# Key sums of two groups in the opening of a four-layer kernel: features on ScalarE, two products in PSUM, masks on GpSimd

## The chip, the core and the metric

The kernel is one program on one NeuronCore of a Trainium2 chip. Its engines are TensorE (PE, with its weight loads PEld), VectorE (DVE), ScalarE (ACT), GpSimd (POOL) and SyncE (SP, which here issues most DMAs). Each engine takes its instructions in program order and waits at semaphores. The metric is the device time of one execution in microseconds, lower is better.

## What is computed

There are 16 sequences of 128 tokens with 256 channels (`x`), and a context of the same shape. Four blocks follow one another, each with a residual and a tanh gate:

```python
x = x + tanh(g_xattn[0]) * L0_xattn(layernorm(x), ctx)   # WKV scan over tokens
x = x + tanh(g_ffn[0])   * L0_ffn(layernorm(x))          # MLP + product-key experts (PEER)
x = x + tanh(g_xattn[1]) * L1_xattn(layernorm(x), ctx)   # linear attention, 16 heads
x = x + tanh(g_ffn[1])   * L1_ffn(layernorm(x))          # 8 experts, top 2, + a shared one
```

The change touches the key side of the linear attention, which depends on the context and on weights alone and so can be computed at any time before the attention:

```python
kvp = kv @ Wkv.T;  k, v = split(kvp, 2)
k = where(k > 0, k + 1.0, exp(k))               # features
kv_summary = einsum('bhsd,bhse->bhde', k, v)    # per head, over the tokens
k_sum = k.sum(axis=-2)
```

## The kernel before

The 16 sequences are handled in four groups of four. `wkv_*` works in WKV groups (0, 1, 2, 3 hold sequences 0 to 3, 8 to 11, 4 to 7, 12 to 15); `mlp`, `attn` and `moe` in main groups.

**The order** is written out by hand. `START` (line 128) is a list of steps `kind group part`, then come four passes `("mlp", f)`, one for each main group, of 12 units and a tail, and `PLAN` (line 133) names the steps that follow each unit. `LAST` closes. Every engine walks the same list `SCHED` and issues its own share of each step, so the list fixes the order on every engine and in every DMA queue. The opening is what stands before the first unit: layer norms, the scans of groups 0 and 1 (`wkv_in`, `wkv_out`), the high and low parts of the first weight blocks (`split`), and a little of `kv`.

**`kv g t`** makes the key sums of one sequence. PE multiplies context by `wkv` into a PSUM bank (L766: key and value, two matmuls of 128x512 in fp32). ACT reads it three times (L1022 to L1024): `k_e` = exp(k), `k_r` = relu(k), and the values into `v_x`, which has 8 columns of ones behind each 128. DVE forms min(k_e, 1) + k_r in place (L1266). At the next part, PE multiplies `k_e` by `v_x` (L775, two matmuls of 128x136, 16 heads' products and the sums at once), and DVE takes the result out of PSUM times `head_mask` into `kv_sum` (L1272), since only the blocks of one head with itself are wanted. `k_e`, `k_r` and `v_x` have two buffers each.

In the list before, sequence 0 and the keys of sequence 1 stand in the opening; group 0 is finished behind units 1 and 2 of the first MLP; group 1 stands behind units 8 to 10 and the start of the second MLP; group 2 behind units 1 to 5 of the second; group 3 behind its units 9 to 12.

**What surrounds it.** An MLP unit below 8 is twelve fp32r matmuls of 512 columns (L636 to L638: three passes, two halves, A and B), a Silu on ACT (L1098), a product on DVE (L1390), and `down` three units later (L660). From unit 8 on the PEER part needs the routes: a long DVE chain (`route g 2` to `8`, L1279 to L1343) ends in transposes and in `exps_t_l` (L1361), for which PE waits with L726. The same DVE queue carries the scans (L1237), reciprocals (L1249), residuals (L1205), layer norm statistics (L1179) and the normalized input (L1201). POOL computes the reciprocal root (L1601, L1596), the low parts of weights (L1566) and parts of the scan's output (L1610 to L1618). PE uses six PSUM banks `ring` in turn. SP loads contexts 2 and 3 behind `kv 0 4` and `kv 1 4`, with `wqg` and `wo` behind the latter, and a weight block behind every `split`.

## Time and profile before

| | us |
|---|---|
| three runs | 518.77, 519.91, 523.19 |
| median | 519.91 |
| span of the profiled execution | 517.5 |

Engine busy time in that span, and the span in 40 slices of 12.9 us:

```profile
PE 449.8 (87%) x2142; PEld 355.1 (69%) x2142; DVE 360.9 (70%) x1034; ACT 246.7 (48%) x452; POOL 154.5 (30%) x156
## 2 busy tenths in 40 slices
PE   1617999599999889999999999898999799899991
PEld 1315688368578666878778886787777588788851
DVE  6896779995289986565987966978867554531173
ACT  3618574363576346346125315470453454955540
POOL 3955342330002131110000001032336014477771
PEclk9966999799999989999999999999999999999997
```

Each digit is the busy share of a slice in tenths; PEclk is the granted clock of TensorE. The first three or four slices are the opening, where PE stands at 1, 6, 1 and 7 tenths while DVE works; from the fifth slice to the last but a few PE is at 9, with gaps at slices 8 (5 tenths) and 14 and 15 (8 tenths). The first unit of the first MLP starts at 43.4 us.

### The profile page before, as it was taken

To read this page: it belongs to the slowest core of one execution; us is meant where nothing else is said; L and a number is where in the kernel's file an instruction comes from. 1 tells how busy PE (TensorE), PEld (TensorE's weight loads), DVE (VectorE), ACT (ScalarE), POOL (GpSimd) and SP (SyncE) were. 2 spreads that over 40 slices of the span, in tenths; PEclk is the share of its full clock that TensorE was granted. 3 is DMA by queue.
4 is the path that set the end of the run, shared out by engine and by line. 5 is a ranking of instruction groups with operands and counts; after the bars stand their busy time and mean duration, and the time that the engine had idled before them with its cause. 6 is when DMAs were issued, how large, how long until landed. Compare 5 with 4: busy or idle time off the path is not lost. (4 is left out here: it accounts for less than half of the span.)

```text
span 517.5 us, 7233 instructions
## 1 busy us (share of the span) xinstructions
PE 449.8 (87%) x2142; PEld 355.1 (69%) x2142; DVE 360.9 (70%) x1034; ACT 246.7 (48%) x452; POOL 154.5 (30%) x156
## 2 busy tenths in 40 slices
PE   1617999599999889999999999898999799899991
PEld 1315688368578666878778886787777588788851
DVE  6896779995289986565987966978867554531173
ACT  3618574363576346346125315470453454955540
POOL 3955342330002131110000001032336014477771
PEclk9966999799999989999999999999999999999997
DMA  8500312000300000960000000123232423346394
GB/s 303 187 31 30 103 31 83 0 1 0 101 2 0 2 0 14 310 178 0 1 1 1 1 0 2 32 71 102 90 115 83 123 73 91 114 139 208 85 385 153
DMA packets 32965, 42.00 MB, mean 81 GB/s; under 512 B 3483, under 2 KB 26781, under 8 KB 32928
## 3 DMA queue, kind: packets, MB, share of 16 engines
q1 hardware_dynamic: 28224, 32.28, 20.7%
q0 software_dynamic: 3744, 8.42, 4.4%
q10 hardware_dynamic: 960, 0.86, 0.5%
q8 instruction: 18, 0.29, 0.2%
q14 instruction: 19, 0.16, 0.1%
HBM read 24.97 MB, written 18.39 MB: 84 GB/s over the span
## 5 line engine op out<-in xcount | busy, mean ns | idle before, releaser
L660 PE MATMUL acc<-w_down,act_s 128*128 128x256 f32 x384 | 92.2, 387 | 0.9 <-DVE act_s L1386 0.9
L660 PEld LDWEIGHTS acc<-w_down,act_s 128*128 128x128 f32 x384 | 74.6, 195 | 13.2 <-DVE act_s L1386 1.3
L636 PE MATMUL ring<-xt_h,up_l 128*128 128x512 f32 x160 | 70.5, 441 | 2.9 <-DVE xt_l L1356 1.5
L1601 POOL TENSOR_TENSOR rstd<-var_eps,minus_half 128x4 f32<-128x4 f32 x14 | 14.9, 1068 | 176.5 <-DVE var_eps L1186 176.5
L637 PE MATMUL ring<-xt_l,up_h 128*128 128x512 f32 x160 | 63.8, 399 | 0.0
L638 PE MATMUL ring<-xt_h,up_h 128*128 128x512 f32 x160 | 63.7, 398 | 0.0
L1098 ACT ACTIVATE act_s<-ring 128x512 f32<-128x512 f32 x48 | 28.6, 597 | 59.9 <-PE ring L638 59.6
L631 PE MATMUL ring<-small,xn 128*128 128x128 f32 x160 | 23.6, 297 | 26.2 <-ACT xn L998 14.1
L699 PE MATMUL ring<-up_e,act_s 128*128 x184 | 44.3, 383 | 2.3 <-issue 2.0
L1637 POOL DMA_INDIRECT x_rows<-main_a,slots x32 | 31.1, 971 | 43.7 <-ACT main_a L1119 34.8
L1390 DVE TENSOR_TENSOR act_s<-ring,act_s 128x512 f32<-128x512 f32 x32 | 22.0, 686 | 30.8 <-PE ring L638 21.0
L631 PEld LDWEIGHTS ring<-small,xn 128*128 128x128 f32 x160 | 20.1, 153 | 29.6 <-ACT xn L998 14.9
L699 PEld LDWEIGHTS ring<-up_e,act_s 128*128 128x128 f32 x184 | 33.1, 190 | 7.1 <-issue 3.5
L636 PEld LDWEIGHTS ring<-xt_h,up_l 128*128 128x128 f32 x160 | 30.5, 191 | 10.5 <-DVE xt_l L1356 1.8
L638 PEld LDWEIGHTS ring<-xt_h,up_h 128*128 128x128 f32 x160 | 30.5, 191 | 7.3
L637 PEld LDWEIGHTS ring<-xt_l,up_h 128*128 128x128 f32 x160 | 30.6, 191 | 7.0 <-issue 1.4
L1098 ACT ACT_TABLE_LOAD x21 | 26.9, 1283 | 0.4
L1205 DVE SCALAR_TENSOR_TENSOR x_nat<-ring,small,x_nat 128x512 f32<-128x512 f32 x24 | 18.0, 749 | 11.2 <-PE ring L893 7.7
L1179 DVE BATCH_NORM_STATS2 stats<-x_nat 128x6 f32<-128x256 f32 x64 | 22.4, 413 | 4.7 <-DMA x_nat<-in_x 4.3
L1645 POOL DMA_INDIRECT y_rows<-act_s,block_home x16 | 15.9, 994 | 30.3 <-ACT act_s L1156 25.6
L726 PE MATMUL ring<-exps_t_l,sel_exps 128*128 128x512 f32 x24 | 13.5, 564 | 9.9 <-DVE exps_t_l L1361 5.3
L1543 DVE TENSOR_TENSOR pairs<-ring,pairs 128x256 f32<-128x256 f32 x12 | 5.1, 423 | 23.3 <-ACT pairs L1139 23.3
(275 smaller groups left out, 987.8 us busy)
## 6 DMA issues: line engine op xcount, KB each, us to landing
main_b<-x_rows SPq DMA_DIRECT2D x22, 257.0 KB, 2.8
x_rows<-v_t SPq DMA_DIRECT2D x1, 3983.5 KB, 16.7
up_l<-y_rows SPq DMA_DIRECT2D x5, 512.0 KB, 7.0
stage<-in_w_mlp SPq DMA_DIRECT2D x8, 256.0 KB, 2.6
up_e<-in_w_moe SPq DMA_DIRECT2D x8, 256.0 KB, 2.6
x_rows<-v_t SPq DMA_DIRECT2D x1, 1927.5 KB, 22.8
x_nat<-in_x SPq DMA_DIRECT2D x7, 256.0 KB, 7.7
out_x<-x_nat SPq DMA_DIRECT2D x6, 256.0 KB, 5.2
```

Of the source, the lines that this page charges most:

```text
L631: last = pe.transpose(bank[:, t * P:(t + 1) * P], xn[n % 2][:, t, c * P:(c + 1) * P], ident)
L636: pe.matmul(out, wl, xh, start=first, stop=False, skip_group_check=True)
L637: pe.matmul(out, wh, xl, start=False, stop=False, skip_group_check=True)
L638: return pe.matmul(out, wh, xh, start=False, stop=final, skip_group_check=True)
L660: last = pe.matmul(acc[t // 2][:, t % 2, :], act_s[n % RING][:, tok], w_down[:, u, :], start=u == 0 and t % 2 == 0, stop=final, skip_group ...
L699: last = pe.matmul(bank[:, j * 2 * P:(j + 1) * 2 * P], x_block_t[n % 2][:, c, j * P:(j + 1) * P], up_e[:, bass.ds(e * UP + c * 2 * P, 2 * ...
L1098: act.activation(act_s[n % RING][:, :], bank[:, :], ACT.Silu).then_inc(free_sem((step, "A", u)), 1)
L1179: last = dve.bn_stats(stats[:, n, t, :], x_nat[:, b, :])
L1205: return dve.scalar_tensor_tensor(out, bank, gates[:, gate:gate + 1], out, ALU.mult, ALU.add)
L1390: free((step, "B", u), dve.tensor_tensor(s[:, :], bank[:, :], s[:, :], ALU.mult))
L1637: pool.indirect_dma_start(x_rows[group_of(g)], bass.IndirectOffsetOnAxis(ap=slots[:, t, k:k + 1], axis=0), to_send[n % SENDS], None).then_ ...
L1645: pool.indirect_dma_start(y_rows, bass.IndirectOffsetOnAxis(ap=block_home[:, n, j:j + 1], axis=0), y_blocks[n % RESULTS][:, j * D:(j + 1) ...
```

## The change

The list of `kv` steps moves one stage ahead: groups 0 and 1 (`OPEN_KV = 2`) are both finished in the opening, group 2 takes the places of group 1, and the places that group 2 had in the second MLP stay empty. `split 0 0` and `split 0 1` stand later in the opening. For the first two groups the features are made on ACT alone, and PE adds the two halves in PSUM. For all groups ACT takes the product out of PSUM unmasked, and POOL applies the mask in `kv_sum` afterwards, in new steps `mask`.

```diff
+OPEN_KV = 2
-START = """wkv_in 0 0, setup 0 0, wkv_in 0 1, wkv_in 1 0, wkv_in 0 2, split 0 0, wkv_out 0 0, wkv_in 1 1, wkv_out 0 1, wkv_in 1 2,
-    wkv_out 0 2 3, split 0 1, kv 0 0, wkv_out 0 4 5, kv 0 1, wkv_out 1 0, wkv_out 0 6 7, x_stats 0 0, wkv_out 1 1, mlp_in 0 0 1,
-    wkv_out 1 2, mlp_in 0 2, wkv_out 1 3 4"""
+START = """wkv_in 0 0, setup 0 0, wkv_in 0 1, wkv_in 1 0, wkv_in 0 2, wkv_out 0 0, kv 0 0, wkv_in 1 1, kv 0 1, wkv_out 0 1,
+    wkv_in 1 2, wkv_out 0 2, kv 0 2, wkv_out 0 3 4, kv 0 3, wkv_out 0 5, split 0 0, kv 0 4, kv 1 0, split 0 1, kv 1 1,
+    wkv_out 1 0, wkv_out 0 6 7, kv 1 2, x_stats 0 0, wkv_out 1 1, kv 1 3, mlp_in 0 0 1, kv 1 4, wkv_out 1 2, mlp_in 0 2,
+    wkv_out 1 3 4"""
...
-        2: "wkv_out 1 6 7, x_stats 1 0, kv 0 2",
+        2: "wkv_out 1 6 7, x_stats 1 0, mask 0 0 1 2 3",
...
@@ PE, kind kv @@
+                        opening = g < OPEN_KV
+                        if opening:
+                            pe.wait_ge(open_k_ready, n + 1)
+                        else:
+                            pe.wait_ge(k_ready, n - OPEN_KV * GT + 1)
...
+                            own = slice(c * P, (c + 1) * P)
+                            last = pe.matmul(bank[:, c * KVW:(c + 1) * KVW], k_e[n % 2][:, own], v_x[n % 2][:, c, :],
+                                             start=True, stop=not opening)
+                            if opening:
+                                last = pe.matmul(bank[:, c * KVW:(c + 1) * KVW], k_r[n % 2][:, own], v_x[n % 2][:, c, :],
+                                                 start=False, stop=True)
@@ ACT, kind kv @@
+                        if g < OPEN_KV:
+                            act.activation(k_e[n % 2][:, :], bank[:, 0:D], ACT.Relu, scale=-1.0).then_inc(k_clipped, 1)
+                        else:
+                            act.activation(k_e[n % 2][:, :], bank[:, 0:D], ACT.Exp)
...
+                        if g < OPEN_KV:
+                            act.wait_ge(k_clipped, n + 1)
+                            act.activation(k_e[n % 2][:, :], k_e[n % 2][:, :], ACT.Exp, scale=-1.0).then_inc(open_k_ready, 1)
+                    if t > 0:
+                        bank = full(act, (step, "V", t - 1))
+                        act.activation(kv_sum[:, wkv_seqs(g)[t - 1], :], bank[:, 0:C * KVW],
+                                       ACT.Copy).then_inc(free_sem((step, "V", t - 1)), 1)
@@ DVE @@
-                        free((step, "V", t - 1), dve.tensor_tensor(
-                            kv_sum[:, seqs[t - 1], :].rearrange("p (c m) -> p c m", c=C),
-                            bank[:, 0:C * KVW].rearrange("p (c m) -> p c m", c=C),
-                            head_mask.unsqueeze(1).broadcast_to([P, C, KVW]), ALU.mult))
+                elif kind == "kv" and g >= OPEN_KV and part < GT:
...
@@ POOL @@
+                elif kind == "mask":
+                    own = kv_sum[:, wkv_seqs(g)[part], :].rearrange("p (c m) -> p c m", c=C)
+                    pool.wait_ge(later_loaded, 16)
+                    freed(pool, (("kv", g), "V", part))
+                    pool.tensor_tensor(own, own, head_mask.unsqueeze(1).broadcast_to([P, C, KVW]),
+                                       ALU.mult).then_inc(sums_masked, 1)
```

exp(-relu(-k)) is min(exp(k), 1), so that `k_e` and `k_r` together are the same feature as before. The masks of group 0 stand behind unit 1 and those of group 1 behind unit 4 of the first MLP, those of groups 2 and 3 behind units 1 and 11 of the second. PE waits for all 16 masks once, at the first attention.

How the order moves, at three places. ACT at the end of the opening, before: `er_pad` and `xt_f_pad` are scan data of group 1, `xn` is the input of the first MLP, `xt_h` its transposed high part.

```order
L984 ACTIVATE xt_f_pad<-xt_f_pad,own_weight 128x4x128
L998 ACTIVATE xn0<-x_nat,shift2,rstd2 128x256 x4
L984 ACTIVATE er_pad<-er_pad,own_weight 128x4x128
L1014 ACTIVATE xt_f_pad<-xt_f_pad,own_weight 128x4x128
L1051 ACTIVATE xt_h<-ring3 128x512
L1051 ACTIVATE xt_h<-ring4 128x512
L1014 ACTIVATE er_pad<-er_pad,own_weight 128x4x128
```

The same place of ACT now, from the features of the last sequence on:

```order
L1038 ACTIVATE k_e1<-ring1 128x256
L1041 ACTIVATE k_r1<-ring1 128x256
L1042 ACTIVATE v_x1<-ring1 128x2x128
L1046 ACTIVATE k_e1<-k_e1 128x256
L1049 ACTIVATE kv_sum<-ring2 128x272
L1012 ACTIVATE xn0<-x_nat,shift2,rstd2 128x256 x4
L1049 ACTIVATE kv_sum<-ring5 128x272
L998 ACTIVATE er_pad<-er_pad,own_weight 128x4x128
L1028 ACTIVATE xt_f_pad<-xt_f_pad,own_weight 128x4x128
L1076 ACTIVATE xt_h<-ring3 128x512
L1076 ACTIVATE xt_h<-ring4 128x512
L1028 ACTIVATE er_pad<-er_pad,own_weight 128x4x128
```

Two sequences of features came in ahead of `xn` (one is shown), and one eviction of `kv_sum` between `xn` and what follows.

PE behind the first unit of the second MLP, before (`q_pad` and `gate_pad` hold the route's input):

```order
L775 MATMUL ring4<-v_x0,k_e0 128x136 x2
L775 MATMUL ring5<-v_x1,k_e1 128x136 x2
L785 MATMUL ring0<-q_pad,later 128x512
L785 MATMUL ring0<-gate_pad,later 128x512
L766 MATMUL ring1<-wkv,v_t0 128x512
L766 MATMUL ring1<-wkv,v_t1 128x512
L636 MATMUL ring2<-xt_h,up_l 128x512
```

Now:

```order
L785 MATMUL ring0<-v_x0,k_e0 128x136 x2
L785 MATMUL ring1<-v_x1,k_e1 128x136 x2
L798 MATMUL ring2<-q_pad,later 128x512
L798 MATMUL ring2<-gate_pad,later 128x512
L641 MATMUL ring3<-xt_h,up_l 128x512
```

The key product of group 2 is gone between the route's product and the next unit.

DVE at the same stretch, before (L1279 begins the route's chain):

```order
L1272 TENSOR_TENSOR kv_sum<-ring4,later 128x272
L1272 TENSOR_TENSOR kv_sum<-ring5,later 128x272
L1266 SCALAR_TENSOR_TENSOR k_e0<-k_e0,k_r0 128x256
L1390 TENSOR_TENSOR act_s1<-ring3,act_s1 128x512
L1279 MAX top_v<-logits1 128x8 x8
L1283 MAX_INDEX top_i<-top_v,logits1 128x8 x8
L1285 TENSOR_TENSOR pairs<-top_v 128x256
L1288 MAX pair_top<-pairs 128x8 x4
L1266 SCALAR_TENSOR_TENSOR k_e1<-k_e1,k_r1 128x256
L1272 TENSOR_TENSOR kv_sum<-ring0,later 128x272
L1390 TENSOR_TENSOR act_s2<-ring2,act_s2 128x512
```

Now:

```order
L1404 TENSOR_TENSOR act_s1<-ring4,act_s1 128x512
L1293 MAX top_v<-logits1 128x8 x8
L1297 MAX_INDEX top_i<-top_v,logits1 128x8 x8
L1299 TENSOR_TENSOR pairs<-top_v 128x256
L1302 MAX pair_top<-pairs 128x8 x4
L1404 TENSOR_TENSOR act_s2<-ring1,act_s2 128x512
```

All evictions of `kv_sum` left DVE, and the features of group 2 no longer stand inside the route's chain.

## Rows read from the trace of the kernel before

**Rows 1.** Busy time by stretch; columns start:end, length, then each engine (instructions), clock, DMA.

```profile
28.00:42.00 14.00, 3.94 (x16) 3.14 (x16) 11.47 (x21) 4.60 (x9) 6.40 (x7) 0.56 0.09 29
...
68.00:96.00 28.00, 23.48 (x117) 19.45 (x115) 26.27 (x76) 14.22 (x21) 10.38 (x8) 0.98 0.17 53
...
142.00:176.00 34.00, 34.00 (x157) 26.83 (x156) 30.56 (x92) 20.25 (x30) 5.27 (x4) 1.00 0.00 1
...
190.00:260.00 70.00, 68.85 (x335) 54.68 (x334) 48.17 (x149) 31.90 (x50) 6.07 (x7) 1.00 0.34 93
```

**Rows 2.** Timeline of PE in the opening: start, duration, instruction, count, idle before.

```profile
18.97 5.59 PE L766 MATMUL ring<-wkv,v_t 128*128 128x512 f32 x8
...
29.80 1.97 PE L752 MATMUL ring<-small,main_a 128*128 128x128 f32 x8 [4.26 <-POOL main_a L1618]
...
43.42 0.77 PE L636 MATMUL ring<-xt_h,up_l 128*128 128x512 f32 x1 [1.46 <-DVE xt_l L1356]
```

**Rows 3.** Timeline of PE after the opening, one sequence's two products.

```profile
53.02 1.88 PE L766 MATMUL ring<-wkv,v_t 128*128 128x512 f32 x4
54.74 0.63 PE L775 MATMUL ring<-v_x,k_e 128*128 128x136 f32 x4
55.12 0.48 PE L636 MATMUL ring<-xt_h,up_l 128*128 128x512 f32 x1
```

**Rows 4.** Timeline of ACT in the opening.

```profile
22.63 0.38 ACT L1022 ACTIVATE k_e<-ring 128x256 f32<-128x256 f32 x1 [0.95 <-PE ring L766]
22.91 0.38 ACT L1023 ACTIVATE k_r<-ring 128x256 f32<-128x256 f32 x1
...
37.87 2.07 ACT L998 ACTIVATE xn<-x_nat,shift,rstd 128x256 f32<-128x256 f32 x4 [5.16 <-POOL shift L1599]
...
41.15 0.60 ACT L1051 ACTIVATE xt_h<-ring 128x512 fp32r<-128x512 f32 x1
```

**Rows 5.** Timeline of DVE in the first MLP.

```profile
58.30 0.69 DVE L1390 TENSOR_TENSOR act_s<-ring,act_s 128x512 f32<-128x512 f32 x1 [1.17 <-PE ring L638]
59.02 1.74 DVE L1201 TENSOR_SCALAR xn<-x_nat,mean_rstd,rstd 128x256 f32<-128x256 f32 x4
...
70.89 1.11 DVE L1279 MAX8 top_v<-logits 128x8 f32<-128x64 f32 x8 [0.55 <-ACT logits L1041]
```

**Rows 6.** Timeline of POOL: the last product of the scan, a reciprocal root, and a 256-wide subtraction.

```profile
50.76 1.27 POOL L1618 TENSOR_TENSOR er_pad<-er_pad 128x512 f32<-128x512 f32 x1 [0.65 <-DVE er_pad L1249]
...
56.53 1.13 POOL L1601 TENSOR_TENSOR rstd<-var_eps,minus_half 128x4 f32<-128x4 f32 x1 [3.27 <-DVE var_eps L1186]
...
108.75 0.73 POOL L1566 TENSOR_TENSOR up_l<-stage,up_h 128x256 fp32r<-128x256 f32 x1
...
153.24 1.11 POOL L1601 TENSOR_TENSOR rstd<-var_eps,minus_half 128x4 f32<-128x4 f32 x1 [38.52 <-DVE var_eps L1186]
```

**Rows 7.** Timeline of PE in the second MLP.

```profile
137.71 1.88 PE L766 MATMUL ring<-wkv,v_t 128*128 128x512 f32 x4
...
142.23 1.05 PE L793 MATMUL ring<-later,logits 128*128 128x128 f32 x8
...
182.43 0.47 PE L726 MATMUL ring<-exps_t_l,sel_exps 128*128 128x512 f32 x1 [3.82 <-issue]
```

**Rows 8.** Timeline of DVE: scans in the opening and later, two places of the second MLP.

```profile
12.08 6.56 DVE L1237 TENSOR_TENSOR_SCAN main_b<-decay,main_a 128x516 f32<-128x516 f32 x4
...
89.13 2.36 DVE L1237 TENSOR_TENSOR_SCAN main_b<-decay,main_a 128x516 f32<-128x516 f32 x2
...
144.02 1.11 DVE L1279 MAX8 top_v<-logits 128x8 f32<-128x64 f32 x8 [0.82 <-ACT logits L1041]
...
154.71 0.69 DVE L1390 TENSOR_TENSOR act_s<-ring,act_s 128x512 f32<-128x512 f32 x1 [0.87 <-DVE kv_sum L1272]
```

**Rows 9.** Groups of DVE after 43 us: line, operation, count | busy us, mean ns | idle before.

```profile
L1272 DVE TENSOR_TENSOR kv_sum<-ring,later 128x272 f32<-128x272 f32 x15 | 6.5, 434 | 1.4 <-DVE kv_sum L1272 0.8 <-PE ring L775 0.5
L1266 DVE SCALAR_TENSOR_TENSOR k_e<-k_e,k_r 128x256 f32<-128x256 f32 x14 | 5.8, 418 | 11.3 <-ACT v_x L1024 11.2
```

More of the change, by code:

```diff
@@ L460, in build @@
         k_ready = sem("k_ready")
+        k_clipped = sem("k_clipped")
+        open_k_ready = sem("open_k_ready")
+        sums_masked = sem("sums_masked")
         diff_ready = sem("diff_ready")
@@ L774, in _ @@
                         for c in range(C):
-                            last = pe.matmul(bank[:, c * KVW:(c + 1) * KVW], k_e[n % 2][:, c * P:(c + 1) * P],
-                                             v_x[n % 2][:, c, :], start=True, stop=True)
+                            own = slice(c * P, (c + 1) * P)
[4 more added lines that the diff above has]
+                                                 start=False, stop=True)
                         close_bank(key, last)
@@ L841, in _ @@
                         once("attn", attn_loaded, 32)
+                        once("masked", sums_masked, NSEQ)
                         for c in range(C):
@@ L1014, in _ @@
                     act.activation(own, own, ACT.Copy, scale=own_weight[:, c:c + 1]).then_inc(own_scaled, 1)
-                elif kind == "kv" and part < GT:
+                elif kind == "kv":
                     t = part
                     n = g * GT + t
-                    bank = full(act, (step, "K", t))
-                    if n >= 2:
-                        prev = divmod(n - 2, GT)
-                        full(act, (("kv", prev[0]), "V", prev[1]))
-                    act.activation(k_e[n % 2][:, :], bank[:, 0:D], ACT.Exp)
-                    act.activation(k_r[n % 2][:, :], bank[:, 0:D], ACT.Relu)
-                    act.activation(v_x[n % 2][:, :, 0:P], bank[:, D:].rearrange("p (c m) -> p c m", c=C),
-                                   ACT.Copy).then_inc(free_sem((step, "K", t)), 1)
+                    if t < GT:
+                        bank = full(act, (step, "K", t))
+                        if n >= 2:
+                            prev = divmod(n - 2, GT)
+                            full(act, (("kv", prev[0]), "V", prev[1]))
+                        if g < OPEN_KV:
+                            act.activation(k_e[n % 2][:, :], bank[:, 0:D], ACT.Relu, scale=-1.0).then_inc(k_clipped, 1)
+                        else:
+                            act.activation(k_e[n % 2][:, :], bank[:, 0:D], ACT.Exp)
+                        act.activation(k_r[n % 2][:, :], bank[:, 0:D], ACT.Relu)
+                        act.activation(v_x[n % 2][:, :, 0:P], bank[:, D:].rearrange("p (c m) -> p c m", c=C),
+                                       ACT.Copy).then_inc(free_sem((step, "K", t)), 1)
+                        if g < OPEN_KV:
[5 more added lines that the diff above has]
+                                       ACT.Copy).then_inc(free_sem((step, "V", t - 1)), 1)
                 elif kind == "split":
@@ L1624, in _ @@
                                        ALU.subtract).then_inc(qg_low, 1)
+                elif kind == "mask":
[4 more added lines that the diff above has]
+                                       ALU.mult).then_inc(sums_masked, 1)
                 elif kind == "clear":
-                    pool.wait_ge(k_ready, NSEQ)
+                    pool.wait_ge(k_ready, NSEQ - OPEN_KV * GT)
                     pool.memset(spare_row[:, 0:D], 0.0)
```

16 lines of the change are left out of this document (4 added, 12 removed), and 22 rows, old and new, of the table PLAN.

## The prediction

> **What bounds the kernel now.** I read the busy shares first, then the stretches, then the timelines of the engines at the places where `kv` stands. TensorE is at 87% of the span, but the opening leaves it at 1 to 7 tenths, so a key product there could be free. Which engine holds the rest changes by stretch [rows 1]. From 68 to 96 us DVE is busy 26.27 of 28 us, and PE, with 23.48, waits for it. From 142 to 176 us PE is busy for all of 34.00 us and DVE for 30.56. Right behind it PE stands still for 3.82 us before L726 at 182.43 [rows 7]: `exps_t_l`, the end of DVE's route chain, is late. So the second MLP is not bound by PE alone; there are two nearly equal queues, and DVE ends last. From 190 to 260 us PE is busy 68.85 of 70 us, and a shift made before it is carried on.
>
> **Prices.** One key product costs PE 54.74 - 53.02 = 1.72 us, one product of features and values 55.12 - 54.74 = 0.38 us [rows 3]. On DVE a feature costs 0.418 us and an eviction with mask 0.434 us [rows 9]. ACT issues a read of 128x256 every 22.91 - 22.63 = 0.28 us and one takes 0.38 us [rows 4], so the four operations of a feature are about 1.1 us. The eviction of 128x272 on ACT isn't in the trace; it lies between that 0.38 us and the 0.60 us of a 512-wide copy [rows 4], and I take 0.4, as 272 is nearest to 256. A mask on POOL isn't there either: a two-input operation of 128x256 takes 0.73 us [rows 6], so 0.73 x 272/256 = 0.78 us, at least 0.73 and at most the 1.27 us of 512 columns [rows 6].
>
> **The opening: 0 us, from -1.5 to +3.** PE gets six more key products and seven more feature products, all eight of the latter doubled: 8 x (1.72 + 2 x 0.38) = 20 us at the full rate, with some 4 us of transposes, between 11 and 42 us. It fits if the clock is up. The eight records of two key products took 5.59 us at 18.97, where 2 x 1.72 = 3.4 us is the full rate [rows 2, 3], and from 28 to 42 us, with PE busy 3.94 of 14 us, the granted clock was 0.56 of full [rows 1]: today the opening runs partly at 1.2 GHz, behind idle stretches. In the new order PE has the first transposes and then two key products without a pause, so I expect 2.4 GHz from about 16 us on. ACT gets 8 x 1.5 = 12 us in place of 2 x 0.9, and DVE loses two features and one eviction. Carried through by hand with these prices, ACT has the features of sequences 0 to 7 ready at about 16, 19, 23, 25, 29, 31, 35 and 37 us; it is free at 37.4, and `xn` started at 37.87 because POOL's shift came then [rows 4]. POOL isn't late for it, since both low parts of weights stand behind the scan's product. What is late next is the last eviction: it stands between `xn` and `xt_h`, and PE makes its product only after the transposes of `xn`, at about 42. The eviction (0.4) and two scan scalings (1.3) then put `xt_h` at 43.4 in place of 41.15 [rows 4], and the first unit at about 45.2 in place of 43.42 [rows 2]. I cost these 1.8 us at nothing: PE had to wait at 52.1 for POOL's product that ends at 50.76 + 1.27 = 52.03 [rows 6], and the 24 matmuls in between took 7.2 us partly at 1.2 GHz; at 2.80/12 = 0.233 us each (from 139.43 to 142.23, [rows 7]) they take 5.6 and end at 50.8. If PE had gone cold again, the cover is gone and 1 to 1.5 us come out. DVE's reciprocals behind `xt_l` move by 1.5 us too, and were free for 1.6 us of that time.
>
> **First MLP: +0.3 us.** Behind unit 1 one key and one feature product stood ahead of unit 2: 2.10 us of PE [rows 3]. DVE's product of unit 2 waited 1.17 us for PE, to 58.30, and the normalized route input could start only at 59.02 [rows 5]. Now it waits for the reciprocal root, 56.53 + 1.13 = 57.66 [rows 6]: 1.4 us earlier, and the logits at 70.89 with it [rows 5]. Everything from there to 96 us is DVE's own work with nothing removed. Behind units 8 to 10 group 2 simply replaces group 1. Against this stand eight masks on POOL behind units 1 and 4, beside a saturated DVE. DVE's scans show what that costs: 6.56/4 = 1.64 us each with POOL at work beside them, 2.36/2 = 1.18 without [rows 8], so 0.46/1.64 = 0.28 us lost for each us. Eight masks are 6.2 us, and lose 6.2 x 0.28 = 1.7 us. Net -1.4 + 1.7 = +0.3, from -1.4 (no loss) to +4.8 (each blocks DVE for its whole length).
>
> The Trainium skill, SBUF — State Buffer, section "SBUF: two separate sides", says that GpSimd and a DVE operation with two SBUF inputs take a shared port pair exclusively, for whole instructions. By this rule the eight masks would cost DVE up to 6.2 us here and the sum would be -0.8 us. The scans speak for less: 4 x 0.46 = 1.8 us lost in 6.56 us [rows 8].
>
> **Second MLP: -5.6 us.** PE loses four key and four feature products: 4 x 2.10 = 8.4 us. It gets less, as DVE ends last. DVE's chain starts earlier by the one key product that stood ahead of the logits (137.71 to 142.23, [rows 7]; start at 144.02, [rows 8]): 1.72 us. Inside the chain go three features and four evictions, 3 x 0.418 + 4 x 0.434 = 2.99 us [rows 9], and the wait of 0.87 us for a PE that is now ahead [rows 8]. 1.72 + 2.99 + 0.87 = 5.6 us earlier at L726; PE then stands there 3.82 + 8.4 - 5.6 = 6.6 us. The masks of group 2 fall where POOL was idle for 38.52 us up to 153.24 [rows 6] and DVE waited for PE, so they cost nothing; if they ran inside the chain, 4 x 0.78 x 0.28 = 0.9 us. Eight fewer changes of ACT's table (the built programs have 52 and 44 loads) shorten nothing on the path; ACT isn't the last.
>
> **Behind it: 0.** Group 3 keeps its places, PE is the bound, the masks were done long before the first attention. In SP's queue contexts 2 and 3 and the attention weights move ahead of the weight blocks of the first MLP; each of these waits for a low part that POOL makes in the MLP, after the moved loads were issued in the opening, so no block is late by them.
>
> Sum: 0 + 0.3 - 5.6 = -5.3 us. Against the profiled execution that is a span of 512.2 in place of 517.5. The median of the runs stands 2.4 us above that span; carried over, 519.91 - 5.3 = 514.6 us.
>
> **The rivals.**
> *PE's saving comes through whole.* If DVE's chain sped up more than I count (fewer collisions, PE ahead everywhere), the end would move by PE's work: 6 key and 7 feature products, 6 x 1.72 + 7 x 0.38 = 13.0 us, so 507 us, and anything between. For it: PE is at 34.00 of 34. Against it: the 3.82 us at L726, where PE waits already. 0.15.
> *The opening gives it back.* ACT's queue puts features ahead of the scan's scalings, and each link from PE to ACT to PE has a latency that my count rounds off. Half a us at each of eight sequences is 4 us at the start of the first MLP; 2.5 to 4 us reach the end: 517 to 518.5. For it: `xn` had 5.16 us of waiting ahead of it, of which I use nearly all. 0.14.
> *POOL's masks block DVE fully.* 6.2 in place of 1.7: 519.1 us. For it: one group of masks stands beside the route chain. Against it: the scans [rows 8]. 0.10. It is what the rule of the Trainium skill's page SBUF — State Buffer, named above, would give.
> *Slower: the clock stays down in the opening.* If PE's pauses while it waits for ACT keep it at 1.2 GHz, the opening costs 8 x (3.44 + 1.52) + 8 = 48 us from 11 on, and ends at 59 in place of 42: +17, so about 531 us. It turns slower than 1% once the opening ends 10.5 us late, that is, once more than half of the products run slow. For it: the granted clock of 0.56 from 28 to 42 us [rows 1], where eight transposes took 1.97 us [rows 2]. Against it: two products in a row at 18.97 took 5.59 us and not the 6.9 us of 1.2 GHz, so the clock rose within them. 0.09.
> That leaves 0.52 for the forecast, with its own range of 512 to 517.
>
> **Numbers.** A measurement of this kernel tells about 1% (5.2 us) from no change. The forecast lies almost on that line, at 514.6 against 514.7; I give it six tenths below the line, since my count of DVE's saving is of work removed and leaves out collisions that go with it. Faster: 0.31 + 0.15 = 0.46. Within 1%: 0.21 + 0.14 + 0.10 = 0.45. Slower: 0.09. The range reaches from the whole saving of PE, 507, to the blocked DVE with some delay of the opening, 520, and leaves the cold opening out.
>
> **What the profile would show.** The first matmul of L641 at 44 to 46 us and granted clock 1.00 in the opening from the second slice on; the wait in front of the first scan output (L757) short. The logits' maximum (now L1293) of group 0 near 70 us if the masks cost little. In the second MLP the wait of PE at L731 longer than before, 6 to 7 us, with DVE without pauses from about 142 us; a wait of 4 us or less there would say that DVE sped up with PE. The first L641 unit after 43 us later than 47 would prove the opening wrong, and DVE operations of double length beside L1643 the price of the masks. A difference that arises behind 260 us is in no step of mine.

## The result

| | before | after |
|---|---|---|
| median, us | 521.22 | 526.06 |
| span of the profiled execution | 517.5 | 524.5 |

The ratio after to before is 1.0096, with a 95% interval of 1.0068 to 1.0124. The change costs 4.8 us, where 5.3 us were to be gained. By the 1% line of the prediction this is "within 1%", but the interval leaves no doubt of the sign. The predicted 514.6 us is 11.5 us too low, and the range ends at 520.

The page of after: busy times, and busy tenths by slice for PE and DVE, with the granted clock.

```profile
PE 457.5 (87%) x2166; PEld 360.8 (69%) x2174; DVE 356.9 (68%) x1010; ACT 242.9 (46%) x468; POOL 167.2 (32%) x172
...
PE   2886599579998869999989999898999699899991
...
DVE  6974829998449985755987966978867454521173
PEclk9997879889999979999999999999999899999996
```

PE's busy time grew by 7.7 us although the change adds it little more than 3 us of products: it worked slowly in places. POOL has 12.7 us more, the 16 masks. PE reads 6 and 5 tenths in the fourth and fifth slice, from 39 to 66 us, where it read 7 and 9 before: there it waits. DVE reads 2 tenths in the sixth, where it read 7: there it waits for a PE that is busy.

### The profile page after: what moved, and what is told of

Read it like the earlier page. It is cut to its first block and busy times, and to the rows that moved or that the text cites. A ratio compares the mean times of both kernels' runs of the same rounds, so it can differ in the third digit from the quotient of the medians.

```text
span 524.5 us, 7302 instructions
## 1 busy us (share of the span) xinstructions
PE 457.5 (87%) x2166; PEld 360.8 (69%) x2174; DVE 356.9 (68%) x1010; ACT 242.9 (46%) x468; POOL 167.2 (32%) x172
## 5 line engine op out<-in xcount | busy, mean ns | idle before, releaser
L665 PE MATMUL acc<-w_down,act_s 128*128 128x256 f32 x384 | 90.8, 383 | 0.9 <-DVE act_s L1400 0.9
L641 PE MATMUL ring<-xt_h,up_l 128*128 128x512 f32 x160 | 72.3, 452 | 5.0 <-DVE xt_l L1370 3.6
L642 PE MATMUL ring<-xt_l,up_h 128*128 128x512 f32 x160 | 65.2, 408 | 0.0
L643 PE MATMUL ring<-xt_h,up_h 128*128 128x512 f32 x160 | 64.9, 406 | 0.0
L704 PE MATMUL ring<-up_e,act_s 128*128 x184 | 45.6, 391 | 2.3 <-issue 2.1
L731 PE MATMUL ring<-exps_t_l,sel_exps 128*128 128x512 f32 x24 | 14.2, 591 | 10.6 <-DVE exps_t_l L1375 9.8
```

The lines of the kernel that those rows point to most:

```text
L641: pe.matmul(out, wl, xh, start=first, stop=False, skip_group_check=True)
L642: pe.matmul(out, wh, xl, start=False, stop=False, skip_group_check=True)
L643: return pe.matmul(out, wh, xh, start=False, stop=final, skip_group_check=True)
L665: last = pe.matmul(acc[t // 2][:, t % 2, :], act_s[n % RING][:, tok], w_down[:, u, :], start=u == 0 and t % 2 == 0, stop=final, skip_group ...
L704: last = pe.matmul(bank[:, j * 2 * P:(j + 1) * 2 * P], x_block_t[n % 2][:, c, j * P:(j + 1) * P], up_e[:, bass.ds(e * UP + c * 2 * P, 2 * ...
```

## Profile after: where the time went

I follow four marks that both kernels have: the first `act_s` on DVE, the logits' maximum (MAX8) and `exps_t_l` of the first MLP, and the same two in the second.

| mark, start in us | before | after | shift | shift since the mark above |
|---|---|---|---|---|
| `act_s` of unit 0 | 48.14 | 50.95 | +2.81 | +2.81 |
| MAX8, first MLP | 70.89 | 77.18 | +6.29 | +3.48 |
| `exps_t_l`, first MLP | 96.11 | 105.69 | +9.58 | +3.29 |
| MAX8, second MLP | 144.02 | 151.87 | +7.85 | -1.73 |
| `exps_t_l`, second MLP | 181.65 | 186.89 | +5.24 | -2.61 |
| first MAX8, third MLP | 227.72 | 233.09 | +5.37 | +0.13 |

**Three losses, two gains.** The end of the table agrees with the medians (4.8 us); what lies behind it differs between single executions by a us or two and isn't read.

*Loss one, the opening.* PE from its last transposes to unit 2, then the transposes of `route_in` and what follows:

```profile
39.80 1.09 PE L636 MATMUL ring<-small,xn 128*128 128x128 f32 x8 [2.63 <-ACT xn L1012]
...
45.38 0.77 PE L641 MATMUL ring<-xt_h,up_l 128*128 128x512 f32 x1 [3.56 <-DVE xt_l L1370]
...
63.59 1.97 PE L636 MATMUL ring<-small,xn 128*128 128x128 f32 x8 [4.79 <-DVE xn L1226]
66.45 3.75 PE L798 MATMUL ring<-main_b,later 128*128 128x512 f32 x4 [0.89 <-ACT main_b L1058]
```

ACT at the same place:

```profile
37.67 2.08 ACT L1012 ACTIVATE xn<-x_nat,shift,rstd 128x256 f32<-128x256 f32 x4
41.86 0.40 ACT L1049 ACTIVATE kv_sum<-ring 128x272 f32<-128x272 f32 x1 [2.11 <-PE ring L788]
...
43.38 1.07 ACT L1076 ACTIVATE xt_h<-ring 128x512 fp32r<-128x512 f32 x2
```

The first unit starts at 45.38, close to the 45.2 that the prediction had. ACT waited 2.11 us for the last value product before it could copy `xt_h`. But PE stood idle for 2.63 us ahead of the transposes and for 3.56 us ahead of the unit, and then started its matmuls every 0.427 us up to 51.5 us; only from there do they follow at 0.233 us. The windows of busy time show it as the granted clock (the columns are those of [rows 1]):

```profile
45.00:52.00 7.00, 6.62 (x16) 5.21 (x17) 4.57 (x5) 4.62 (x10) 4.21 (x4) 0.53 0.07 7
56.00:70.00 14.00, 8.32 (x25) 4.99 (x25) 8.62 (x25) 2.31 (x4) 6.40 (x8) 0.71 0.19 57
```

From 45 to 52 us the clock was 0.53 of full, that is, 1.2 GHz for nearly all of it. Over the 5.57 us to the first `act_s` the kernel before needed 4.72 us.

*Loss two, behind unit 2.* DVE in the first MLP, which answers [rows 5]:

```profile
60.50 3.03 DVE L1226 TENSOR_SCALAR xn<-x_nat,mean_rstd,rstd 128x256 f32<-128x256 f32 x4 [0.64 <-POOL rstd L1615]
...
74.00 0.69 DVE L1404 TENSOR_TENSOR act_s<-ring,act_s 128x512 f32<-128x512 f32 x1 [8.54 <-PE ring L643]
```

The normalized route input starts at 60.50 and takes 3.03 us in place of 1.74. PE, which before had a key and a value product here, is idle for 4.79 us, and after this idle time the transposes take 1.97 us, the products of L798 3.75 us (before, the eight and four records took 1.09 and 1.96), and unit 3 begins slowly. DVE waits 8.54 us for it.

*Loss three, the route chain.* POOL's masks of groups 0 and 1, and the low parts of weights that come next:

```profile
60.34 3.05 POOL L1643 TENSOR_TENSOR kv_sum<-kv_sum,later 128x272 f32<-128x272 f32 x4
...
83.49 3.61 POOL L1643 TENSOR_TENSOR kv_sum<-kv_sum,later 128x272 f32<-128x272 f32 x4
88.11 2.15 POOL L1580 TENSOR_TENSOR up_l<-stage,up_h 128x512 fp32r<-128x512 f32 x2 [1.01 <-ACT up_h L966]
```

DVE beside them:

```profile
83.73 0.75 DVE L1310 TENSOR_TENSOR exps<-logits,top_v 128x32 f32<-128x32 f32 x1
...
85.48 0.99 DVE L1318 TENSOR_TENSOR pair_rep<-pairs,pair_rep 128x256 f32<-128x256 f32 x1
86.50 0.42 DVE L1320 TENSOR_REDUCE r_cnt<-pair_rep 128x32 f32<-128x256 f32 x1
...
88.33 2.22 DVE L1337 TENSOR_TENSOR onehot<-iy_b,key_iota 128x512 bf16<-128x512 bf16 x2
```

`exps` (L1310) took 0.18 us before and takes 0.75 now, the cast 0.18 and 0.62, L1318 0.42 and 0.99. These three are 1.6 us. The reduction at 86.50, with one input, is not longer. L1337 took 0.76 for two and takes 2.22, and its next two (at 93.29) take 1.29: 2.0 us more, beside the low parts. The masks did not push these low parts: POOL waited 1.01 us for ACT's `up_h` ahead of them, and they start 10.9 us behind MAX8, before 10.7. It is DVE that came 1.3 us later to L1337 (11.15 us behind MAX8, before 9.85) and so no longer passed it ahead of the low parts. From MAX8 to `exps_t_l` it is 28.51 us, in place of 25.22.

*The gains,* in the second MLP, DVE first, then PE's wait, which answers the last line of [rows 7]:

```profile
160.76 0.69 DVE L1404 TENSOR_TENSOR act_s<-ring,act_s 128x512 f32<-128x512 f32 x1 [0.67 <-ACT act_s L1123]
...
168.73 2.30 DVE L1337 TENSOR_TENSOR onehot<-iy_b,key_iota 128x512 bf16<-128x512 bf16 x2
```

```profile
187.68 0.77 PE L731 MATMUL ring<-exps_t_l,sel_exps 128*128 128x512 f32 x1 [5.57 <-DVE exps_t_l L1375]
```

The chain starts 1.73 us earlier against what led up to it, and is 35.02 us long in place of 37.63. PE waits 5.57 us for its end, not 3.82.

## The experiments

Every time below is the start of the mark in one profiled execution. Of each ratio to the kernel before, measured beside it on the same chip, the table gives the 95% interval. The chip of the four runs whose names begin with r takes longer over the last part of the program (the kernel before had 535.25 us there), so for those only the ratio and the marks are compared. "Third" is the first MAX8 of the third MLP, behind which nothing differs between the kernels.

| run | `act_s` 0 | MAX8 | `exps_t_l` | MAX8, 2nd | `exps_t_l`, 2nd | third | ratio (interval) |
|---|---|---|---|---|---|---|---|
| before | 48.14 | 70.89 | 96.11 | 144.02 | 181.65 | 227.72 | 1 |
| after | 50.95 | 77.18 | 105.69 | 151.87 | 186.89 | 233.09 | 1.0096 (1.0068-1.0124) |
| c1, after again | 51.71 | 77.18 | 105.70 | 151.87 | 186.89 | 232.84 | 1.0090 (1.0056-1.0123) |
| r1, no masks | 51.40 | 76.06 | 100.98 | 147.16 | 182.18 | 228.22 | 0.9990 (0.996-1.002) |
| r2, filled ahead of unit 2 | 50.01 | 76.03 | 104.53 | 150.70 | 185.73 | 232.94 | 1.0095 (1.0063-1.0128) |
| r3, the same and opening | 48.42 | 75.71 | 104.23 | 150.40 | 185.42 | 231.16 | 1.0053 (1.0028-1.0078) |
| r4, last value late | 46.84 | 72.78 | 101.28 | 147.44 | 182.46 | 228.46 | 0.9987 (0.9959-1.0015) |
| d1, filled opening | 48.54 | 73.95 | 102.46 | 148.61 | 183.66 | 229.38 | 1.0059 (1.0035-1.0083) |
| d2, both gaps filled | 48.61 | 71.32 | 99.83 | 145.98 | 181.03 | 228.13 | 1.0008 (0.9984-1.0032) |
| s1, r4 + gap filled | 46.49 | 70.90 | 99.41 | 145.57 | 180.59 | 227.79 | 0.9990 (0.9965-1.0016) |
| s2, r4 + masks late | 46.61 | 70.99 | 95.91 | 142.08 | 177.12 | 224.41 | 0.9930 (0.9906-0.9954) |
| s3, r4 + group 2 early | 46.07 | 71.43 | 100.47 | 140.89 | 176.39 | 223.23 | 0.9906 (0.987-0.9941) |
| s4, s2 + s3 | 46.57 | 69.52 | 94.73 | 135.18 | 170.21 | 217.89 | 0.9810 (0.9776-0.9844) |
| c4, s4 with an open gap | 45.97 | 70.62 | 95.55 | 141.37 | 176.40 | 223.02 | 0.9919 (0.9891-0.9948) |
| c3, s4, DVE evicts | 51.03 | 73.86 | 99.07 | 139.51 | 174.55 | 221.81 | 0.9881 (0.9846-0.9916) |
| d3, s4, DVE evicts 2, 3 | 46.63 | 69.51 | 94.73 | 135.17 | 170.21 | 217.62 | 0.9802 (0.9753-0.985) |
| c2, old order, masks on POOL | 49.12 | 73.49 | 98.68 | 146.60 | 184.37 | 230.39 | 1.0043 (1.0023-1.0064) |

The theories: **A**, TensorE's clock, which falls in idle stretches that the change opens; **B**, the masks on POOL beside DVE; **C**, ACT's wait for the last value product in front of `xt_h`.

### The masks (r1)

```diff
-        2: "wkv_out 1 6 7, x_stats 1 0, mask 0 0 1 2 3",
+        2: "wkv_out 1 6 7, x_stats 1 0",
...
-                        once("masked", sums_masked, NSEQ)
```

> The changed kernel with the 16 mask products on GpSimd and the wait for them left out, so the sums keep the products of unlike heads. Theory B (the masks take VectorE's time in the first MLP): the normalized input of route_in beside them goes back from 3.03 to about 1.74 us, the route chain from its MAX8 (77.18) to exps_t_l (105.69) from 28.5 back to about 25.2, together 4.5 us, so about 521.5. Theory A (TensorE's clock after the idle stretches is the cause): the normalized input is ready 1.3 us earlier, the first matmuls of units 0 and 3 stay slow, no more than 1.3 us of the total comes back, about 525.

DVE without them (the lines are one lower here):

```profile
60.94 2.22 DVE L1225 TENSOR_SCALAR xn<-x_nat,mean_rstd,rstd 128x256 f32<-128x256 f32 x4 [0.64 <-POOL rstd L1614]
...
82.61 0.18 DVE L1309 TENSOR_TENSOR exps<-logits,top_v 128x32 f32<-128x32 f32 x1
...
85.61 0.76 DVE L1336 TENSOR_TENSOR onehot<-iy_b,key_iota 128x512 bf16<-128x512 bf16 x2
```

And POOL's low parts, which L1336 passes again just ahead of them:

```profile
86.41 2.52 POOL L1579 TENSOR_TENSOR up_l<-stage,up_h 128x512 fp32r<-128x512 f32 x2 [4.01 <-ACT up_h L965]
```

The chain from MAX8 to `exps_t_l` takes 24.92 us, `exps`, cast and L1317 are back at 0.18, 0.18 and 0.42 us, and the third MLP is 4.87 us ahead of after. B has the size it named, 4.5 us. The route input takes 2.22 us, not yet 1.74: a low part of weights on POOL (60.78 to 62.04) stands beside its first half. But A isn't refuted by this, since MAX8 still comes 5.2 us later than before.

### The clock (r2, r3, d1, d2)

The extra products give nothing; they only keep TensorE at work. First ones ahead of unit 2, then also in the opening:

```diff
+                elif kind == "warm":
+                    for c in range(part):
+                        pe.matmul(acc[g].rearrange("p t d -> p (t d)"), wkv[:, 0, 0:P], wkv[:, 1, :],
+                                  start=True, stop=True, skip_group_check=True)
-        2: "wkv_out 1 6 7, x_stats 1 0, mask 0 0 1 2 3",
+        2: "wkv_out 1 6 7, x_stats 1 0, warm 0 4, mask 0 0 1 2 3",
```

> The changed kernel with four extra fp32 products of 128x512 (0.94 us each by the rows of the keys) on TensorE behind unit 2 of the first MLP, into an accumulator that is not yet in use, where the key sums of group 0 stood before: only what TensorE does in its 4.79 us of waiting changes. Theory A: the granted clock stays up, the transposes of route_in take 1.1 and not 1.97 us, unit 3's matmuls are at the short spacing, MAX8 of the first MLP comes at about 74 and not 77.2, total about 523. Theory B: nothing changes at MAX8 but 1 us at most, total 525 to 526.

> As the run with extra products behind unit 2, and five more in the opening: two before the transposes of mlp_in (2.63 us of waiting) and three behind them (3.56 us of waiting). Theory A: the 24 matmuls of units 0 and 1 take 5.6 and not 8.4 us, the Y output of group 0 comes at about 52.1, MAX8 at about 71.5, total about 520. Theory B: the first part of the MLP may come earlier, but the masks still lengthen the chain from MAX8 to exps_t_l to 28.5 us; if only the masks mattered the total would stay at 525 to 526.

I had put those four in the wrong place. The steps named behind a unit stand ahead of the next one, and the gap lies behind unit 2, not ahead of it. They delayed unit 2: its `act_s` came at 61.38 in r2 and at 59.18 in after. MAX8 gained only 1.15 us, and nothing of it reached the end (1.0095). r2 is a miss that tells little; r3 showed that five products in the opening bring `act_s` back to 48.42. The clean pair came later:

```diff
-    kv 1 3, mlp_in 0 0 1, kv 1 4, wkv_out 1 2, mlp_in 0 2,
+    kv 1 3, warm 1 2, mlp_in 0 0 1, kv 1 4, wkv_out 1 2, mlp_in 0 2, warm 1 3,
```

> The changed kernel with five extra fp32 products of 128x512 in TensorE's two waits of the opening and nothing else: the wait of ScalarE for the last eviction stays, only the clock can differ. If the opening's loss at act_s (2.8 us in one profile, 3.6 in the other) is the wait plus the clock, act_s comes at 48.4 as in the run with both gaps filled; behind unit 3 the changed kernel came to 74.0 from either start, so the gain at the end is the open point: 2.5 us (ratio 1.004) if it carries through, 1.009 if the slow stretch just moves behind the next wait.

PE in d1, the extra products (L762), the transposes, the first unit, and the second gap, which stays open; behind it the window that after had at 0.53:

```profile
37.01 1.88 PE L762 MATMUL acc<-wkv 128*128 128x512 f32 x4
39.81 1.09 PE L636 MATMUL ring<-small,xn 128*128 128x128 f32 x8 [0.92 <-ACT xn L1016]
...
41.67 2.74 PE L762 MATMUL acc<-wkv 128*128 128x512 f32 x6
45.40 0.47 PE L641 MATMUL ring<-xt_h,up_l 128*128 128x512 f32 x1 [0.99 <-DVE xt_l L1374]
...
61.17 1.97 PE L636 MATMUL ring<-small,xn 128*128 128x128 f32 x8 [4.79 <-DVE xn L1230]
```

```profile
45.00:52.00 7.00, 5.84 (x24) 4.43 (x24) 6.64 (x6) 5.64 (x12) 5.12 (x5) 1.00 0.18 50
```

The first unit starts at 45.40, no earlier than in after. The clock is 1.00, the 24 matmuls follow at the short spacing, and the first `act_s` comes at 48.54, 2.4 us earlier than in after and 0.4 later than in the kernel before. So the late start is nearly covered while the clock is up, as the prediction said: 0.4 of the 2.8 us are left, and 2.4 are the clock. Covered isn't free: r4, below, has its first unit 1.7 us earlier than d1, and is 1.7 us ahead at `act_s` and 0.9 at the third MLP. The gain of d1 carries through in the profiles, where the third MLP is 3.7 us ahead of after. The ratio falls from 1.009 to 1.0059, which is 1.6 to 1.9 us, and the intervals overlap. I had the size at 2.5 us.

d2 adds four more directly ahead of the transposes of `route_in`:

```diff
-        3: "route_in 0 1 2, route 0 0, wkv_in 2 0",
+        3: "route_in 0 1, warm 0 4, route_in 0 2, route 0 0, wkv_in 2 0",
```

> As above, and four more extra products directly ahead of the transposes of route_in. All of theory A without any other edit: act_s of unit 3 at about 70 (74.0 less 2.5 and 1.9), ratio about 1.001. What is left above the kernel before at the route chain is theory B's, about 4 us.

```profile
56.28 3.59 PE L762 MATMUL acc<-wkv 128*128 128x512 f32 x8
61.25 1.09 PE L636 MATMUL ring<-small,xn 128*128 128x128 f32 x8 [1.38 <-DVE xn L1230]
63.29 1.96 PE L802 MATMUL ring<-main_b,later 128*128 128x512 f32 x4 [0.94 <-ACT main_b L1062]
```

Both prices are back at the values of before, 1.09 and 1.96 us. From the end of the route input (58.16 + 3.04 = 61.20) to MAX8 it is 10.12 us; before it was 59.02 + 1.74 = 60.76 to 70.89, 10.13 us, and in after 63.53 to 77.18, 13.65 us. So the 3.5 us of loss two are the clock, to a tenth. The ratio is 1.0008: nine products whose result nobody reads take back nearly the whole 4.8 us, and here the intervals are apart. A is shown.

### The last value (r4)

```diff
-    kv 1 3, mlp_in 0 0 1, kv 1 4, wkv_out 1 2, mlp_in 0 2,
+    kv 1 3, mlp_in 0 0 1, wkv_out 1 2, mlp_in 0 2, kv 1 4,
```

> The changed kernel with the last part of the opening's key sums (kv 1 4) behind mlp_in 0 2 and not between its parts, so that ScalarE's copies of xt_h do not wait for the last eviction. Theory C (this wait starts the first unit late): the first unit starts at about 43.4 and not 45.4, and the total falls by the same 2 us, about 524. Theory A: TensorE's idle stretch ahead of the first unit gets shorter too, and if the clock stays up for it, 2.8 us more come back at act_s; if it does not, the 2 us alone.

ACT in r4:

```profile
41.42 0.60 ACT L1076 ACTIVATE xt_h<-ring 128x512 fp32r<-128x512 f32 x1
...
43.78 0.40 ACT L1049 ACTIVATE kv_sum<-ring 128x272 f32<-128x272 f32 x1 [0.91 <-PE ring L788]
```

`xt_h` comes at 41.42 and the last eviction behind it. PE, with its transposes, and the first unit:

```profile
40.27 1.97 PE L636 MATMUL ring<-small,xn 128*128 128x128 f32 x8 [2.63 <-ACT xn L1012]
...
43.69 0.48 PE L641 MATMUL ring<-xt_h,up_l 128*128 128x512 f32 x1
```

PE's order is the same as in after. Its transposes run slowly, behind the first gap (in the execution of after that has a profile the clock fell later), but the second gap of 3.56 us is gone, the clock is up again by the first unit, and the matmuls follow every 0.23 us. `act_s` comes 4.1 us earlier than in after, and the third MLP 4.6 us. One moved step removes the wait and the cold start together, and the ratio is 0.9987. Theory C had 2 us for the wait. C and A pay for the same place, so d1 and r4 must not be added.

### Real work in the gap, and the masks elsewhere (s1 to s4, c4)

All five start from r4. s1 puts three extra products into the gap ahead of `route_in`; s2 moves the masks of groups 0 and 1 into the second MLP; s3 takes group 2 forward; s4 is s2 and s3; c4 is s4 with the key sums of group 2 all behind units 8 to 11.

s4 against after, without the line of r4. The last two pairs are of the second MLP:

```diff
-        2: "wkv_out 1 6 7, x_stats 1 0, mask 0 0 1 2 3",
-        3: "route_in 0 1 2, route 0 0, wkv_in 2 0",
+        2: "wkv_out 1 6 7, x_stats 1 0",
+        3: "route_in 0 1, kv 2 0, route_in 0 2, kv 2 1, route 0 0, wkv_in 2 0",
...
-        5: "route 0 4 5 6, mask 1 0 1 2 3",
+        5: "route 0 4 5 6",
...
-        9: "wkv_out 2 4 5, kv 2 0",
-        10: "wkv_out 2 6 7, x_stats 2 0, kv 2 1",
-        11: "mlp_in 1 0, kv 2 2",
+        9: "wkv_out 2 4 5, kv 2 2",
+        10: "wkv_out 2 6 7, x_stats 2 0, kv 2 3",
+        11: "mlp_in 1 0, kv 2 4",
...
-        1: "mlp_out 0 0, kv 2 3 4, route 1 0",
-        2: "route 1 1 2 3, mask 2 0 1 2 3",
+        1: "mlp_out 0 0, route 1 0",
+        2: "route 1 1 2 3, mask 2 0 1, mask 0 0 1 2 3, mask 2 2 3, mask 1 0 1 2 3",
```

> The run with the last value late, and three extra fp32 products of 128x512 on TensorE directly ahead of the transposes of route_in, where a key and a value product of group 0 stood before (in the two runs with filled gaps they stood a unit too early, ahead of unit 2, and delayed it). The control is the run with the last value late: xn of route_in ready at 59.9, act_s of unit 3 at 69.6, ratio to before 0.999. Theory A (idle TensorE ahead of these transposes lets its clock fall for what follows): half speed leaves the stretch from 60 to 67, act_s of unit 3 comes at about 67.2, ratio about 0.994. Against it: the stretch stays slow or the 2.4 us are eaten by the route chain behind, ratio 0.999.

> The run with the last value late, and the masks of groups 0 and 1 behind those of group 2 in the second MLP, where GpSimd waits for long. Theory B: xn of route_in takes about 2.3 and not 3.03 us, the chain from MAX8 (72.8) to exps_t_l (102.0) falls from 29.2 to about 25.5, ratio about 0.990. If the masks only fill time in which VectorE's own chain is not what TensorE waits for, the ratio stays at 0.999.

s1 gains 1.9 us up to `exps_t_l` of both MLPs and 0.7 us at the third; its ratio, 0.999, is that of r4. The other 1.2 us are lost right behind PE's wait for `exps_t_l` of the second MLP, at the same eight `down` products, in r4 and then in s1:

```profile
185.55 2.44 PE L665 MATMUL acc<-w_down,act_s 128*128 128x256 f32 x8
...
183.67 3.62 PE L665 MATMUL acc<-w_down,act_s 128*128 128x256 f32 x8
```

PE is at 1.2 GHz behind that wait in both, and in s1 for longer: the granted clock from 184 to 188 us is 0.60, in r4 0.67. I have no run that changes the clock there alone. s2 gains 5.4 us at `exps_t_l` and 4.05 at the third, ratio 0.993, most of what theory B asked (0.990). From `exps_t_l` to the next MAX8, where its eight masks now lie, it takes 46.17 us against 46.16 in r4: there they cost nothing.

> The run with the last value late, and the key sums of group 2 two parts further ahead: kv 2 0 ahead of and kv 2 1 behind the transposes of route_in, the rest behind units 8 to 10, none in the second MLP before its route chain. Theory A: real work in the gap does what the extra products do, act_s of unit 3 at about 67.5; the second MLP's route chain gains about 1 us more; ratio about 0.992. Against it: VectorE's feature operations beside xn cost as much as the clock gives, ratio 0.999.

> Both edits: the masks of groups 0 and 1 in the second MLP, and group 2 two parts further ahead. If A and B are separate and add, the ratio is about 0.983; if they pay the same wait, it is that of the better one alone, 0.990.

PE in s4, at the place where it had idled for 4.79 us:

```profile
58.45 1.09 PE L636 MATMUL ring<-small,xn 128*128 128x128 f32 x8 [2.27 <-DVE xn L1226]
...
61.56 1.88 PE L798 MATMUL ring<-main_b,later 128*128 128x512 f32 x4
```

The transposes take 1.09 us and L798 1.88. The gap still has 2.27 us of waiting, and the clock stays up. In s3, with the same order of PE here but the masks still beside `xn`, it did not:

```profile
58.71 1.97 PE L636 MATMUL ring<-small,xn 128*128 128x128 f32 x8 [3.09 <-DVE xn L1226]
```

So one key product ahead of the transposes holds the clock in one profile and not in the other. The two edits do not pay the same wait: at the third MLP s2 gains 4.05 us on r4, s3 5.2 and s4 10.6, somewhat more than the sum. s4 is at 510.13 us against 521.50 of the kernel before, 1.9% faster, and faster than the forecast of the change itself. More than the clock is in it. From `exps_t_l` to the next MAX8 it is 40.4 us in s3 and s4 (135.18 - 94.73 and 140.89 - 100.47), where after and r4 have 46.2. PE is busy for 43.9 of these 46.2 us in r4, and makes all four key products of group 2 there. In s3 and s4 two of them and one product of features and values stand ahead of `exps_t_l`, where PE waits for DVE anyway: 2 x 1.72 + 0.38 = 3.8 us of work [rows 3], and PE's wait of 1.10 us for a feature is gone too. Together this is 4.9 of the 5.7 us.

> The masks late and the last value late, and the key sums of group 2 all behind units 8 to 11 of the first MLP: the second MLP has none before its route chain, as in the fastest run, but the gap ahead of route_in's transposes stays empty. Theory A says that filling the gap is worth 1.5 to 2 us (s1 got 1.9 at act_s of unit 3): act_s of unit 3 at 67.8 as with the masks late alone, total 1.5 us above the fastest, ratio about 0.984. If the gap is worth nothing at the end, ratio 0.981; if the second MLP's empty start is not what gained 5 us there, 0.993.

c4 doesn't separate the gap as I wanted. It loses 1.1 us at MAX8 for the open gap (1.7 counted from `act_s`), near what I gave it, and another 5.4 us up to the next MAX8:

```profile
100.66 3.60 PE L771 MATMUL ring<-wkv,v_t 128*128 128x512 f32 x8
107.14 0.73 PE L785 MATMUL ring<-v_x,k_e 128*128 128x136 f32 x4 [2.89 <-DVE k_e L1288]
```

All four key products of group 2 are between `exps_t_l` and the next MAX8 again, which is 3.8 us of work, and PE waits 2.89 us for a feature there, where s4 waits 1.39 us for POOL. That is 5.3 of the 5.4 us. The second MLP of c4 has no key sum ahead of its route chain, as in s4, and so its empty start is not what s4 gained by; the work moved ahead of `exps_t_l` is. Its ratio, 0.992, is not the price of the gap.

### Who evicts (c2, c3, d3), and the control (c1)

> The changed kernel itself, beside the other runs of this call, as their control: ratio 1.0096 as before. Its first act_s came at 50.95 us in the one profile so far, and at 50.0 in the kernel that is equal to it up to there (extra products behind unit 1); if the clock's falls in the opening differ from one execution to the next, it can be anywhere in 50 to 51, with the same shift of about 5 us behind 228.

c1 repeats after in both: ratio 1.009, and all marks from MAX8 on within 0.3 us, though `act_s` came 0.8 us later. Where the clock falls in the opening differs from one execution to the next.

c2 has the order of before and of the change only the eviction by ACT and the masks on POOL.

```diff
-OPEN_KV = 2
+OPEN_KV = 0
...
+        3: "route_in 0 1, kv 0 3, route_in 0 2, kv 0 4, mask 0 0 1 2 3, route 0 0, wkv_in 2 0",
```

> The order of the kernel before (OPEN_KV 0, features with VectorE, group 0 in the first MLP and so on), and of the change only that ScalarE takes the product out of PSUM and GpSimd masks it, right behind each group's last part. Theory B (the masks cost VectorE more than its evictions did): the 16 evictions of 0.44 us leave VectorE, the masks of group 0 run beside the route chain of the first MLP and add some 2 us there; total slower than before by 1 to 2 us, ratio 1.002 to 1.004. If handing the eviction away is a gain by itself, as the forecast had it (0.28 us lost for 0.76 us of mask against 0.44 us saved), ratio 0.997 to 1.000.

c2 is slower, 1.0043 (theory B had 1.002 to 1.004). Its route input (59.97) takes 3.40 us beside POOL, 1.7 more than before, and the chain behind it is as long as before. The other 1.0 us of its 2.6 at MAX8 arises ahead of the first `act_s`, where its granted clock from 45 to 52 us was 0.73 and before 0.87. In the second MLP 4 x 0.434 = 1.7 us of evictions left DVE's chain [rows 9], and the chain took 37.77 us in place of 37.63: what DVE lost in work came back mostly as waits for `act_s` (1.45 us for ACT and 0.53 for PE). Handing the eviction away is no gain by itself.

c3 has the order of s4, and VectorE evicts and masks as before; d3 does so for groups 2 and 3 alone.

> The fastest order so far (last value late, group 2 two parts further ahead), with VectorE evicting and masking from PSUM as in the kernel before, no mask on GpSimd and no copy on ScalarE; features of the first two groups stay on ScalarE. If ScalarE's eviction in the opening is what the order needs (VectorE is the engine that ends the opening), 8 evictions of 0.45 us come on top of its chain, up to 3.6 us later at act_s, ratio about 0.987 to 0.990. If it does not matter who evicts as long as no mask lies beside the route chain, ratio 0.981 as with the late masks.

In the opening it matters: in c3, with the evictions on DVE, `xn` starts at 41.33 (38.13 in r4), `act_s` comes 4.5 us later than in s4, the ratio is 0.988, as expected. With VectorE as the evictor throughout, the new order is still worth 1.2%.

> The fastest kernel so far, with ScalarE's evictions and GpSimd's late masks for the two groups of the opening alone, and VectorE evicting and masking groups 2 and 3 from PSUM as in the kernel before. VectorE takes 8 evictions of 0.44 us back where TensorE is the bound, and its xn in the second MLP goes from 2.96 to 1.38 us beside no masks: within 1 us of the fastest, ratio 0.979 to 0.983. If evictions on VectorE in front of act_s cost as those of the opening did, 0.985.

d3 and s4 are the same within their intervals, 0.9802 and 0.9810. The split belongs in the opening only; for groups 2 and 3 either will do.

## Why the prediction failed

*The opening: 0 forecast, +2.8 measured.* The start of the first unit was right (45.2, measured 45.38), and so was the cause, the last eviction between `xn` and `xt_h`. The step that failed is "I cost these 1.8 us at nothing", with the 24 matmuls at 0.233 us each. The prediction asked for 2.4 GHz from 16 us on and had it: the clock was 1.00 from 28 to 42 us. It didn't ask what PE does between its last product and the first unit. It had itself counted the start of `xn` and the late `xt_h`, and between these PE has nothing to do but eight transposes and one doubled product. The 2.6 and 3.6 us of idle time could be read from the tally, and the sentence "if PE had gone cold again, the cover is gone" names the case without giving it the weight. It also put the price too low: 1 to 1.5 us, where d1 shows 2.4 at `act_s` and, in the profiles, 3.7 at the third MLP.

*The first MLP: +0.3 forecast, +6.8 measured.* Two parts. The 1.4 us for the products taken from unit 2's front were right: the route input starts 9.55 us behind the first `act_s`, before 10.88. What was left out is the next pair, behind unit 2: it stood in a stretch where PE waits for DVE anyway. Taking it out gained nothing and cost 3.5 us of clock (d2). The masks were put at 1.7 us and cost 1.29 + 3.29 = 4.6 us, for 3.05 + 3.61 = 6.66 us of POOL's time: 0.69 us for each us, not 0.28. r1 gives 4.9. The scans, from which 0.28 came, were the wrong row. Beside the masks themselves DVE lost 1.29 us at the normalization and 1.58 at three short operations, 0.44 to 0.57 each, 2.9 us in all and 0.43 for each us; other short operations passed. The rest is a term that the sum did not have: DVE, late by the masks, ran into the low parts of weights (2.0 us, less 0.3 at another place).

The Trainium skill, SBUF — State Buffer, section "SBUF: two separate sides", has the shared port pair locked for whole instructions, against VectorE operations with two SBUF inputs or in a two-port mode. By the prediction's estimate that would have been up to 6.2 us here. The runs come nearer to this sum (4.6 to 4.9 us) than to that of the scans, though partly through the low parts. The reduction at 86.50, with one input, passed a mask at its usual length, which fits the rule. This was the third rival, at 0.10; with its price in place the forecast would have been about 517.5.

*The second MLP: -5.6 forecast, -4.35 measured.* The earlier start was exact (1.72, measured 1.73). Of the 3.86 us inside the chain 2.61 came. Three features and four evictions did leave (3.0 us). The wait of 0.87 us shrank to 0.67 and not to 0: the profile now names ACT at it, and [rows 8] had not named PE either, so "PE that is now ahead" was the wrong releaser. And POOL's product for the scan, which had lain beside L1326 and lengthened it by 1.0 us, now lies beside L1337 and lengthens that by 1.5. 3.0 + 0.2 - 0.5 = 2.7. PE's wait, forecast at 6.6, is 5.57 us.

*Behind it: 0.* That holds, +0.13 us up to the third MLP.

*Rivals.* None is what happened. "The opening gives it back" had the right place with another mechanism; the slower rival had the right mechanism in a form that would need half of the opening. Three small losses of one direction make the sum, and no rival had two of them.

## What to carry to other kernels

Work that TensorE does while it waits for another engine is not only free, it can hold the clock for what comes next: before moving it away, look at how long TensorE then idles in front of a chain that others wait for, and price what follows at half speed. Cost a helper engine's operation beside VectorE by the operations that it will really meet, ask what a VectorE that is late by it runs into next, and put it where no engine waits for VectorE. Work of the bounding engine gains most when it moves from a stretch where that engine is the bound to one where it waits. An edit that fails may need only its order changed: the same idea with one step moved, the masks late and real work in the gap is 1.9% faster than the kernel before.
